# Moving VectorE's dense weight sums behind the value units, and GpSimd's low parts of the value weights' sums forward

## The reference, cut to what matters

```python
x = x + attn(layernorm(x))        # x: 2 x 1024 x 1024, f32
x = x + ffn(layernorm(x))
# attn: conv of width 3 to 3*256 channels, split into q, k, v (256 each)
#   blocks of 128 tokens, 16 heads of 64: qh = q@wq+bq, kh = k@wk+bk, vh = v@wv+bv
#   p = softmax(causal(qh*kh/8)); o = p@vh; (o@wo + bo) @ proj_w + proj_b
# ffn: y = x@W_base.T + b_base, plus four experts of rank 8,
#   weighted by softmax(log(prior) + x@router_W.T + router_b)
```

## Time and profile before

| | us |
|---|---|
| median of 3 runs | 767.96 (767.40 to 769.08) |
| the profiled execution's own time | 767.93 |
| its span | 766.2 |
| TensorE matmuls busy | 745.9 |
| VectorE busy | 584.6 |
| ScalarE busy | 458.7 |
| GpSimd busy | 186.1 |

### The profile page before, as it was taken

One profiled execution on the slowest core, in us unless ns is written; L12 is line 12 of the kernel. 1 busy time (PEld: TensorE's weight loads), 2 busy tenths in 40 slices (PEclk: granted clock), 3 DMA queues, 4 the chain that ended last, 5 costly groups with the idle time before them and its releaser, 6 DMA issues.

```text
span 766.2 us, 15175 instructions
## 1 busy us (share of the span) xinstructions
PE 745.9 (97%) x5311; PEld 670.7 (88%) x5311; DVE 584.6 (76%) x1573; ACT 458.7 (60%) x1189; POOL 186.1 (24%) x212
## 2 busy tenths in 40 slices
PE   4999999999999999999899999999999999999997
PEld 3898888888888889999899998999988899999997
DVE  6999996879888885767876776576688567777784
ACT  5963443334433787788677777777794155566530
POOL 2300100000000123645462626253430211222200
PEclk9999999999999999999999999999999999999999
DMA  8836843444445244163536364513357986433402
GB/s 323 300 119 188 259 118 130 173 165 145 165 143 215 111 167 118 56 205 104 177 101 212 89 218 155 188 48 111 114 195 224 353 219 208 134 124 134 159 29 83
DMA packets 64848, 124.12 MB, mean 162 GB/s; under 512 B 11908, under 2 KB 32516, under 8 KB 63365
## 3 DMA queue, kind: packets, MB, share of 16 engines
q1 hardware_dynamic: 62756, 115.81, 45.9%
q0 software_dynamic: 2016, 7.34, 2.4%
HBM read 87.92 MB, written 34.80 MB: 160 GB/s over the span
## 4 chain that ended last, share of the span: by engine, by line
PE 87%; DVE 5%; DMA 3%; ACT 3%; issue 1%; SPq 0%; DVEq 0%; ACTq 0%
PE net_psum L63 13%; PE net_psum L65 13%; PE net_psum L64 13%; PE net_psum L1941 11%; PE net_psum L2224 5%; PE net_psum L2226 5%; PE net_psum L2225 5%; PE net_psum L2043 4%; PE net_psum L2055 4%; PE net_psum L2067 3%; PE net_psum L2097 2%; PE net_psum L2098 2%; PE net_psum L2099 2%; DMA t_scratch<-t_low 1%; PE net_psum L1925 1%
## 5 line engine op out<-in xcount | busy, mean ns | idle before, releaser
L784 POOL TENSOR_TENSOR pr<-pr,rrec 128x512 f32<-128x512 f32 x64 | 66.5, 1042 | 195.3 <-DVE rrec L1426 194.2
L971 ACT ACTIVATE pr<-pr,negmax 128x128 f32<-128x128 f32 x256 | 99.6, 400 | 1.3 <-DVE negmax L1418 1.3
L1941 PE MATMUL net_psum<-ua,wa 128*128 128x256 f32 x384 | 83.8, 379 | 0.6 <-DVE ua L1308 0.6
L1941 PEld LDWEIGHTS net_psum<-ua,wa 128*128 128x128 f32 x384 | 72.6, 190 | 10.4 <-issue 0.8
L928 ACT ACTIVATE w_hi<-raw 128x1024 fp32r<-128x1024 f32 x24 | 25.5, 1063 | 85.4 <-PE net_psum L65 76.7
L63 PE MATMUL net_psum<-x_hi,w_hi 128*128 128x512 f32 x192 | 76.4, 398 | 0.0
L64 PE MATMUL net_psum<-x_lo,w_hi 128*128 128x512 f32 x192 | 76.2, 397 | 0.0
L65 PE MATMUL net_psum<-x_hi,w_lo 128*128 128x512 f32 x192 | 75.6, 394 | 0.0
L63 PE MATMUL net_psum<-c_hi,wqk_hi 128*128 128x256 f32 x256 | 74.1, 289 | 0.0
L64 PE MATMUL net_psum<-c_lo,wqk_hi 128*128 128x256 f32 x256 | 71.6, 280 | 0.0
L65 PE MATMUL net_psum<-c_hi,wqk_lo 128*128 128x256 f32 x256 | 71.5, 279 | 0.0
(11 more groups left out here) (302 smaller groups left out, 2309.9 us busy)
## 6 DMA issues: line engine op xcount, KB each, us to landing
wa<-in_conv_w SPq DMA_DIRECT2D x24, 512.0 KB, 4.1
raw<-in_conv_w SPq DMA_DIRECT2D x24, 384.0 KB, 4.5
xn<-in_x SPq DMA_DIRECT2D x16, 512.0 KB, 10.5
xr<-in_x SPq DMA_DIRECT2D x8, 1024.0 KB, 5.6
x_scratch<-xr SPq DMA_DIRECT2D x8, 1024.0 KB, 4.5
x1t<-x_scratch SPq DMA_DIRECT2D x16, 512.0 KB, 4.9
x1g<-x_scratch SPq DMA_DIRECT2D x56, 128.0 KB, 3.0
out<-x1t POOLq DMA_DIRECT2D x14, 512.0 KB, 3.3
```

The lines of the kernel that those rows point to most:

```text
L784: pool.tensor_tensor(pr[:, jj % 4], pr[:, jj % 4], rrec[:, jj % 4].unsqueeze(2).to_broadcast([P, UN, P]), ALU.mult).then_inc(s["p_ready"], 1)
L971: e = act.activation(pr[:, jj % 4, un], pr[:, jj % 4, un], ACT.Exp, bias=negmax[:, jj % 2, un:un + 1], scale=-1.0, accum_out=rsum[:, jj % ...
L1941: mm = pe.matmul(duo_acc(d, mi)[:, v * QUADS:(v + 1) * QUADS], wa[:, a % AW, mi, 1 - v, c % 2], ua[:, c, v, n * QUADS:(n + 1) * QUADS], st ...
```

## The change

VectorE: of the sums that are due in a double step, those with k % 4 of 1, 2 and 3 are now in the late call, where before it was k % 4 = 1 alone. So the sums of q = 1 (k % 4 = 2) and q = 2 (k % 4 = 3), in D = 9, 10, 13, 14, 17, 18, 21 and 22, each with the low part of the sum before, go from in front of the first bank's copy to behind the second. The order of the sums among themselves, and with it every count of `t_step`, stays.

GpSimd: the four low parts of the value weights' sums leave D = 12. Two are made in D = 9, two in D = 11, each behind that step's multiplies and `c_low`.

```diff
     def sums_in(D, late):
-        return [k for k in range(TSUMS) if sum_at(k) == D and (k % 4 == 1) == late]
+        return [k for k in range(TSUMS) if sum_at(k) == D and (k % 4 > 0) == late]
...
                 if D == DG * SEVEN - 4:
                     value_weight_sums()
-                if D == DG * SEVEN:
-                    low_value_sums()
+                if D in (DG * SEVEN - 3, DG * SEVEN - 1):
+                    low_value_sums(D - (DG * SEVEN - 3))
...
-            def low_value_sums():
-
-                for i in range(4):
+            def low_value_sums(first):
+
+                for i in (first, first + 1):
                     pool.wait_ge(s["v_high_ready"], WC + i + 1)
                     pool.tensor_tensor(value_sum(1, i), value_raw(i), value_sum(0, i), ALU.subtract).then_inc(s["pool_step"], 1)
```

## The result

The changed kernel takes 778.26 us in the median of four runs (777.27 to 779.23), the kernel before, beside it on the same chip, 768.52 (767.40 to 769.21): a ratio of 1.0128, with a 95% interval from 1.0106 to 1.0150. It is slower, by 1.3%. The forecast was 775.2 with a range up to 777.5: right in sign and in the place of the loss, too small in its size.

The account below looks back on a forecast made before the run. TensorE, busy 97% of the span, was taken to bound the kernel. Terms -2.04 - 0.73 + 0.7 + 9.3 = +7.2 us on 767.93 gave 775.2 us, range 767.2 to 777.5.

Parts of the forecast that it names:

- The low parts on GpSimd, at nothing: Four low parts moved from D = 12 to D = 9 and 11 cost nothing, covered by GpSimd's idle time.
- D = 13, -2.04: With VectorE less blocked, the value copy comes sooner and TensorE's stall goes whole: -2.04 us.
- D = 22, -0.73: The loss in D = 21 to 24 comes from the dense pair ahead of the copy and goes: -0.73 us.
- D = 11, +0.7: The late pair of D = 10 delays a_low, so the projection waits: +0.7 us, bounds 0.3 and 1.0.
- The three stalls, 3.1 each: Late pairs of D = 14, 18, 22, blocked by GpSimd, delay a_low for the next step's projection: +9.3 us.
- Who gets the port first: At D = 14, 18, 22 GpSimd's c_lo goes first, 775.2 us; rival, VectorE first, 768.6 us, chance 0.20.
- The Trainium skill's rule: At the port in D = 14, 18, 22, whichever starts first blocks the other; by it the sum is 775.2 us.

Follow-up runs that it names:

- low_only: The changed kernel with VectorE's pairs back in front of the units, so only GpSimd's four low parts are moved: 765.19 us, ratio 0.9970.
- the looks at the kernel before: The kernel before, run unchanged three more times to see its scatter: 767.33, 766.95 and 768.89 us.
- vec_only: The kernel before with VectorE's sums moved as in the change, GpSimd's four low parts left in D = 12: 779.94 us, ratio 1.0156.
- one_late: The changed kernel with the q = 1 pairs late, but of the q = 2 pairs only that of D = 14: 769.62 us, ratio 1.0006.
- bias_early: The changed kernel with GpSimd's two bias additions made one double step sooner, in q = 2 ahead of the multiplies: 768.91 us, ratio 1.0008.
- port_free: The changed kernel with GpSimd's c_lo of D = 10, 14, 18, 22 held until VectorE's late pair is made: 765.74 us, ratio 0.9974.
- the third look: The last of three further executions of the kernel before, unchanged: 768.89 us.
- filler: The changed kernel with 20 transposes on TensorE ahead of its wait for a_lo in D = 15, 19 and 23: 774.40 us, ratio 1.0077.

## Why the prediction was too low

- **The low parts on GpSimd, at nothing:** right. They come where forecast (from 336.00 and from 356.44), nothing waits for them, and with them alone the kernel gains.
- **D = 13, -2.04:** right. In the changed kernel's timeline the copy starts 0.03 us behind its product's end and ends 1.2 us ahead of the product that needs it:

```profile
369.63 0.40 PE L1978 MATMUL net_psum<-wv_hi,c_lo 128*128 128x512 f32 x1
370.06 0.69 DVE L1455 COPY vf<-net_psum 128x512 f32<-128x512 f32 x1 [0.91 <-PE net_psum L1978]
...
371.96 0.39 PE L1976 MATMUL net_psum<-vt_hi,vs_hi 128*128 128x512 f32 x1
```

  It takes GpSimd's half; VectorE's half alone leaves 0.67.
- **D = 22, -0.73:** the loss went, but it was no fixed cost of the order. "Comes from the dense pair ahead of the copy" is half of it: in that one execution the pair was itself late, by 1.15 us of waiting for a store, and TensorE's wait behind it was 0.32 us with a restart of 0.1. The other 0.3 us isn't accounted for. `low_only` keeps the pair ahead of the copy and has no loss, and the looks at the kernel before have next to none.
- **D = 11, +0.7:** a wait of 0.38, near the lower bound of 0.3. The turns were those forecast: the dense sum through at 343.13 + 1.02 = 344.15, then c_lo until 345.84, the low part until 346.40, a tenth sooner than worked out; the rest lies in TensorE's coming a little later.
- **The three stalls, 3.1 each:** the mechanism held to the tenth and the stalls were 2.66, 2.70 and 2.67. From the value copy to the end of a_low it took 391.65 - 383.62 = 8.03 us where the working has 8.19, and TensorE came to the projection 0.25 later behind the copy than in the earlier trace rows (389.13 - 383.62 = 5.51, against 430.52 - 425.26 = 5.26). The term was 0.4 too large each.
- **The step that failed** is in the same term: "Against 430.40 that is 3.05 us, with the slower restart of some 0.1 (a first matmul of 0.50 in the earlier trace rows) 3.1 us." A stall was priced at its own length and a restart of 0.1. Behind each stall TensorE ran about 3.4 us at half clock, 1.7 us more. The price of a stall was 4.5 us (44.51 - 40.02), and the profile of before, in which the clock stays at full speed behind 1.94 us and first falls at 765.2, when TensorE has ended its work at 760.8, gave no sign of it. The scatter of its runs did.

The sum as it should have been: -2.77, then waits of 0.38 + 2.66 + 2.70 + 2.67 = 8.4, restarts of 4 x 0.1, and 3 x 1.7 = 5.1 for the clock. That is +11.1 us; the profiled executions differ by 11.2. Without the clock it would have been +6.0, 773.9 us, inside the range. In the median of the runs some 0.9 us of this is missing, since two of the four probably had one fall fewer; those two, 777.27 and 777.41, lie just inside the range.

- **Who gets the port first** was the largest doubt, at 0.52 for GpSimd. It went to GpSimd in all three steps, by 0.03 us each time, and again in D = 14 of `vec_only`, `one_late` and `bias_early`.
- **The Trainium skill's rule**, page "SBUF — State Buffer", section "SBUF: two separate sides", that whoever starts first keeps the port pair for the whole instruction and the other is fully blocked: the traces agree at 0.03 us, in every line shown here of a sum of 2.35 us beside c_lo. `port_free` says nothing of who wins, since c_lo is held there until the pair is through; it shows that the pair takes 0.70 each when nothing is in its way.

## What to carry to other kernels

Before moving VectorE work with both inputs in SBUF, lay it beside GpSimd's instructions at the new place and not beside VectorE's idle time: here the same pairs cost 12.5 us or nothing (778.26 against 765.74), by 1.4 us of GpSimd's start. Price a long TensorE wait (here 1.92 us and more; waits up to 0.91 had no fall) at its length plus what the clock may take behind it, and where a kernel's times fall into two groups, look whether the mean granted clocks do too. Try the halves of a change apart: here one of them was worth 0.3% and the other lost 1.6%.

## What was not expected of the hardware

- **The clock falls behind a wait, not in it.** Waits of 2.60 to 2.73 us were followed by half clock in all seven profiled cases (three in the changed kernel, three in `vec_only`, one in `one_late`), beginning 0.05 to 1.2 us after TensorE had started again and costing 1.7 us each. It isn't certain to come: by the times and mean clocks, four of the ten runs of `one_late` went without. The wait of 1.92 to 1.94 us in the kernel before had it in one of four profiled executions, the third look, 0.3 us behind the restart at 373.46. In the first 9.5 us of that kernel's span, ahead of its first matmul, TensorE stands still too, and the clock column reads 1.00 there and behind; no run tells why. The Trainium skill, page "TensorE: Matmul & The Clock Gate", section "Part 1: The HAM clock gate", has TensorE's clock at either 1.2 or 2.4 GHz by how busy the engine has been of late, and the phase of its watch not tied to the program. The two levels are seen here, and one program that falls in some executions and not in others is what such a phase would give; no run here tests it.
- **A wait that is short enough is only a wait.** With 0.40 to 0.91 us of standing still (`filler`, `bias_early`) no fall was seen. In the 53 runs of the six kernels without a long wait the mean granted clock is 0.998 to 1.000 throughout, and none of them has the two groups 1.5 us apart, though single runs stand up to 1.3 us above their kernel's median (`low_only` 766.45 against 765.19).
- **Turns at the port.** Once VectorE's sum had waited for c_lo, its low part did not follow directly: GpSimd's bias addition, waiting by then, went in between, in D = 14, 18 and 22 alike. A pair of some 1.3 us (383.80 to 385.12 in `port_free`) lasted 5.2 (384.22 to 389.40).
